# Two-sided feed-forward and delta-rule attention on one core: the order of four kinds of TensorE work in the expert tiles, and of two ScalarE steps

## The reference

```
scores = softmax(norm(x) @ gate_w)                 # 8 experts, the two best are kept
xs = scale[e, t] * norm(x)[t]                      # per expert
h  = silu(xs @ w1[e]) * (xs @ w3[e])               # 256 -> 128
out = sum over e of h @ w2[e]                      # 128 -> 256
```

## Time and profile before

| what | value |
|---|---|
| median of 3 runs | 1615.22 us (1611.40 to 1615.74) |
| span of the profiled execution, first to last instruction | 1613.1 us |
| the profiled execution's own time | not given apart from its span; the median is 2.1 us above the span |
| first mixture of experts, passes | about 146 to 263 us and 273 to 390 us |
| attention | about 390 to 1333 us |
| second mixture of experts, passes | about 1362 to 1481 us and 1490 to 1613 us |
| mean granted clock of TensorE over the span | 0.909 |

### The profile page before, as it was taken

One profiled execution on the slowest core, in us unless ns is written; L12 is line 12 of the kernel. 1 busy time (PEld: TensorE's weight loads), 2 busy tenths in 40 slices (PEclk: granted clock), 3 DMA queues, 4 the chain that ended last, 5 costly groups with the idle time before them and its releaser, 6 DMA issues. The chain is left out here.

```text
span 1613.1 us, 36942 instructions
## 1 busy us (share of the span) xinstructions
PE 1332.5 (83%) x11688; PEld 1246.2 (77%) x11688; DVE 1153.0 (71%) x3044; ACT 918.2 (57%) x1853; POOL 1004.1 (62%) x1783
## 2 busy tenths in 40 slices
PE   7673994994579999999999999999999851995996
PEld 7673994994468888888888888888888741995896
DVE  6664673673768888879889888798898534673574
ACT  2113772771356676767676767666676413772773
POOL 4762673565366676777776866867768532575366
PEclk8555997998689999999999999999999975998999
DMA  7426976772011212132222231222222245885682
GB/s 209 155 100 175 307 261 220 236 252 68 10 30 39 51 45 70 39 77 72 67 68 50 65 76 39 77 65 66 75 50 59 68 119 163 263 270 185 247 287 85
DMA packets 224026, 195.90 MB, mean 121 GB/s; under 512 B 105556, under 2 KB 186714, under 8 KB 223840
## 3 DMA queue, kind: packets, MB, share of 16 engines
q1 hardware_dynamic: 190560, 117.21, 26.4%
q0 software_dynamic: 24576, 67.94, 11.5%
q10 hardware_dynamic: 8704, 8.39, 1.8%
HBM read 103.68 MB, written 96.10 MB: 124 GB/s over the span
## 5 line engine op out<-in xcount | busy, mean ns | idle before, releaser
L1560 DVE SCALAR_TENSOR_TENSOR raw_w<-attn_raw,taps,raw_w 128x256 f32<-128x256 f32 x576 | 251.8, 496 | 43.4 <-ACT raw_w L1933 43.4
L468 PE MATMUL ffn_both<-ws,ffn_xhi 128*128 x1152 | 203.7, 289 | 0.8 <-issue 0.2
L468 PEld LDWEIGHTS ffn_both<-ws,ffn_xhi 128*128 128x128 f32 x1152 | 164.1, 192 | 3.2 <-issue 3.1
L457 PE MATMUL ffn_both<-ident,ffn_xb 128*128 128x128 f32 x576 | 82.1, 290 | 96.0 <-ACT ffn_xb L752 96.0
L2217 POOL TENSOR_TENSOR attn_inv<-attn_inv,attn_term 64x14 f32<-64x14 f32 (+6 forms) x448 | 135.5, 303 | 35.1
L2214 POOL TENSOR_TENSOR attn_term<-attn_small,attn_inv 64x14 f32<-64x14 f32 (+6 forms) x448 | 130.4, 291 | 35.1
L1201 PE MATMUL attn_fr<-attn_xhi,wqkv 128*128 128x256 f32 x768 | 149.0, 297 | 2.5 <-DVE attn_xlo L1540 1.6
L457 PEld LDWEIGHTS ffn_both<-ident,ffn_xb 128*128 128x128 f32 x576 | 70.0, 150 | 98.3 <-ACT ffn_xb L752 77.4
L1201 PEld LDWEIGHTS attn_fr<-attn_xhi,wqkv 128*128 128x128 f32 x768 | 113.4, 194 | 14.4 <-issue 10.9
L491 PE MATMUL ffn_yb<-ws,ffn_hhi 128*128 x576 | 118.6, 290 | 6.2 <-DVE ffn_hlo L667 6.2
L829 POOL DMA_INDIRECT second_rows<-ffn_more_rows,ffn_to x64 | 63.1, 986 | 85.0 <-DVE ffn_to L652 68.9
(11 more groups left out here) (319 smaller groups left out, 4139.6 us busy)
## 6 DMA issues: line engine op xcount, KB each, us to landing
ffn_more_rows<-second_rows SPq DMA_DIRECT2D x56, 259.0 KB
ffn_xb<-second_rows SPq DMA_DIRECT2D x48, 259.0 KB
raw_w<-second_rows SPq DMA_DIRECT2D x40, 259.0 KB
ffn_more_rows<-first_rows SPq DMA_DIRECT2D x64, 131.0 KB
ffn_xb<-in_L_attn_x_dram SPq DMA_DIRECT2D x8, 1024.0 KB, 5.9
attn_xin<-x_after_first ACTq DMA_DIRECT2D x32, 256.0 KB, 2.7
attn_xres<-x_after_first SPq DMA_DIRECT2D x32, 256.0 KB, 3.0
x_after_attention<-attn_xres SPq DMA_DIRECT2D x32, 256.0 KB, 2.2
```

Of the source, the lines that this page charges most:

```text
L457: last = pe.transpose(tr[:, q, j * P:(j + 1) * P], xs[:, k % 2, j, q * P:(q + 1) * P], ident[:])
L468: last = pe.matmul(hp[:, j, :], (xhi, xlo)[b][:, k % 2, q, j * P:(j + 1) * P], ws[:, bass.ds(experts[j], 1), a, q].rearrange("p o d -> p ( ...
L1560: dve.scalar_tensor_tensor(acc[:, j, r], raw[:, j, r, :, tap:tap + P], taps[:, j, r, tap:tap + 1], acc[:, j, r], ALU.mult, ALU.add)\
```

## The change

On TensorE `down(k-1)` is issued directly behind `up(k)`, and `turn_rows(k+2)` behind it, directly ahead of `turn_hidden(k)`. On ScalarE `high_hidden(k)` is issued ahead of `scaled(k+3)`. The functions themselves, the waits in them, the buffers and the other engines' orders stay as they are.

```diff
@@ -521,10 +521,10 @@   (TensorE)
                 for k in range(start, end):
                     now = table_row(k, 0, mybir.EngineType.PE, E - 1)
                     up(k, now)
+                    if k > start:
+                        down(k - 1, of)
                     if k + 2 < end:
                         turn_rows(k + 2)
-                    if k > start:
-                        down(k - 1, of)
                     turn_hidden(k)
                     of = now
                 down(end - 1, of)
@@ -795,9 +795,9 @@   (ScalarE)
                     silu(k)
                     if k + 2 < end:
                         high_part(k + 2)
+                    high_hidden(k)
                     if k + 3 < end:
                         scaled(k + 3)
-                    high_hidden(k)
                     if first_stage and 11 <= k < 16:
                         round_attention_weights(k)
```

## The result

| | kernel before | changed kernel |
|---|---|---|
| median, four runs each on one chip | 1614.42 us (1611.40 to 1615.74) | 1623.11 us (1622.25 to 1626.77) |
| ratio | | 1.0056, 95% interval 1.0037 to 1.0075 |
| profiled execution | span 1613.1 us | 1622.95 us, span 1621.2 us |
| mean granted clock of TensorE over the span | 0.909 | 0.905 |

The change costs 8.7 us by the medians and 8.1 us by the spans. That is slower by more than the 0.3% which a measurement of this kernel can tell.

What follows compares the result with a forecast made beforehand. TensorE's own work, 5.556 us a pass, was taken to bound the expert stages; 56 waits of 0.105 us make 5.9, less 0.7 of small waits 5.2, so 1615.2 + 5.2 = 1620.4 us, range 1615 to 1626.

Steps and rivals of the forecast that it cites:

- The ring: Loop down(k-1), turn_rows, high_part, low_part, low_hidden, down(k): 5.66 us against TensorE's 5.556, so 0.105 us wait ahead of down.
- The two links that no row of before showed in just this place: VectorE's low_hidden starts 0.09 us before low_part's end; hlo's end to down's first product on TensorE takes 0.20 us.
- The places: Expected signs: xlo directly behind xhi, VectorE idle ahead of xlo and not hlo, TensorE waiting about 0.1 us at down.
- One sign: TensorE idle ahead of L491 (down), about 0.1 us x 56, and a bit under 40.00 in a 40 us window.
- No overlap on VectorE: Rival: low_hidden starts only at low_part's end or 0.03 after; ring 5.75 to 5.78, 1625 to 1627 us; chance 0.12.
- The ring's own forecast: Ring of 5.62 to 5.71 us a pass, total 1618.5 to 1623, centred at 1620.4; chance 0.63.
- No new wait: Rival: hlo to down under 0.10 us, ring at or under TensorE's 5.556, time 1614.5 to 1615; chance 0.17.
- faster: Rival: TensorE saves by products directly behind products and turns behind turns; 0.08 us a pass gives 1610 us; chance 0.05.
- The clock: Rival: TensorE's clock falls with twelve turns in one block; one pass in ten costs 34 us, 1650; chance 0.03.
- How many passes: TensorE waits at downs 1 to 14 of each half: 4 x 14 x 0.105 = 5.9 us, less 0.7, 5.2.
- the slack of ScalarE's edit: Hid done at 1.63, wanted by turn_hidden at 2.39: slack 0.76 us, about 0.2 where attention weights are rounded; no cost.
- the chain of the prediction: ScalarE after the edit: xhi, hhi, four scalings ending at 6.07, silu starting at 5.97, 0.31 us into the next pass.

Runs made afterwards that it cites:

- Experiment 3: Changed kernel with low_hidden(k) ahead of goals(k+2) and low_part(k+2) on VectorE: 1765.7 us, ratio 1.0059, stalled session; repeated without stalls, 1618.44 us, ratio 1.0029.
- `pe_only`: Kernel before with TensorE's edit alone: 1772.8 us in one run, against 1753.1 of the kernel before, in a stalled session.
- Experiment 5: Changed kernel with a 128 x 256 memset added on VectorE between low_part(k+2) and low_hidden(k): 1772.3 us in one run, against 1741.3 of the kernel before, stalled session.
- `after_dve_2`: Second run of Experiment 3's kernel, in a session without stalls: 1618.44 us, ratio 1.0029 to the kernel before.
- experiment 7: Changed kernel with low_hidden ahead of low_part and the next pass's table read directly behind up(k), without stalls: 1611.03 us against 1614.01 before, ratio 0.9985.
- `act_only`: Kernel before with ScalarE's edit alone, run twice in stalled sessions (kernel before 1741 to 1753 us): 1768.4 us, ratio 1.0087, and 1764.3 us, ratio 1.0133.

## Why the prediction was right, and where it fell short

**The ring: right.** The sum was 5.66 us a pass. The trace has 5.63 and 5.67, and each link stands within 0.05 us of its term. The two links that no row of before showed in just this place came out as taken. Low_hidden started 0.07 to 0.09 us ahead of low_part's end in all 64 such pairs, and hlo to down was 0.20. The predicted loss was 5.2 us, and the ring's share is 5.3. Experiment 3 took it away by opening the ring at VectorE, and `pe_only` gave the other length, 6.99. Experiment 5 put a dose into it and moved its last links.

**The places: right.** Xlo stands directly behind xhi in time, VectorE is idle ahead of xlo (0.74 us) and not ahead of hlo, the clock is 1.00 in the windows. One sign was read wrongly beforehand. The prediction looked for idle time ahead of L491 and for TensorE a bit under 40.00 of 40. The page shows 6.2 us before and after, and two of the windows show 40.00: the trace shows the waiting first product of down as running, for 0.38 us in place of 0.28. The pitch behind it and the count of matmuls in a window show the wait.

**The rivals.** No overlap on VectorE would have made 5.75 to 5.78 us a pass; the second choices show 5.63 to 5.68 in nearly all passes. That the total comes near the first end of this rival's 1625 to 1627 us is chance: its mechanism isn't in the trace. The range of 1615 to 1626 reaches that high because of this rival. The ring's own forecast, 1618.5 to 1623, ends where the measured 1623.1 lies, so that the number came out inside the range is in part luck: 3.5 of the 8.7 us come from what wasn't in the sum. The prediction set against its sum a sentence of the Trainium skill (VectorE: DVE Perf Modes, "The DRAIN you can't avoid"), that the next VectorE operation doesn't start until the pipe is empty. The 64 early starts are for the exception that the page makes for an operation that isn't held. No new wait, and faster, fall with the 5.65. The clock didn't fall with twelve turns in a row.

**The total: short by 3.5 us** (5.2 predicted, 8.7 measured). Two steps failed. The first is "How many passes": 4 x 14 waits of 0.105 us at down, as if these were all. The chain that it counts runs through instructions on tiles. The sequencer's read of the expert's number ahead of up isn't in it, nor among the rivals. That read begins only when hid is done, and it has 0.35 us of slack; the kernel before had as little (the read below, from 213.4, ends at 213.76, and up comes at 214.45, 0.69 later, of which 0.37 are needed).

```profile
L345 PEldq TENSOR_LOAD <-tab x1: 358/358/358, 213.4 to 213.4; - x1
```

So in most passes the change didn't shorten the slack. With it more reads are long: 3 over 0.68 us before, and 10 and 12 in the two profiles of the changed kernel, 11 in that of `after_dve_2`.

The second step is the slack of ScalarE's edit: 0.76 us, and "about 0.2 us of slack stays" where the attention weights are rounded. These sizes are right for turn_hidden: hid ends 0.79 us ahead of it, and 0.13 in passes 12 and 14. But the read waits for hid too, and from hid's end to up it needs 0.06 + 0.33 + 0.37 = 0.76 us, where turn_hidden needs 0.36. For the read the slack is 0.35 to 0.4 us, and in these two passes hid comes 0.65 later, which is more than that.

That a read behind hid makes the long passes is shown: with the read a pass ahead they are gone (experiment 7 against `after_dve_2`), those with a long read and those with a late hid. Together they are 1.7 us in the stretches of the changed kernel. How the 1.7 divides is estimated above from the rows of single passes; no run separates the two. Why more reads are long is open. In the kernel before 9 of the 72 reads began while POOL was issuing a store, in the changed kernel 57, among them all ten long ones, with 11 or more of the 16 DMA engines busy. But none of the three long reads of before began in a store, 18 reads of the changed kernel took up to 0.35 us with 13 or more engines busy, and in experiment 7, with 54 reads in stores, only three are long. Traffic may be a part of the cause and isn't shown to be.

The rest, 8.1 - 7.0 = 1.1 us of the spans, lies outside the stretches. From up(16) of the second half to up(1) of the third, where the attention's code is unchanged, it took 1006.86 us before, 1008.54 after, and 1008.87, 1005.82 and 1008.20 in three other kernels. That varies by 3 us among kernels with the same code there, so this rest isn't given a cause. The last 0.6 us are between spans and medians (8.1 and 8.7).

**ScalarE's edit: its cost by itself is open.** The prediction gave it none, alone or with the other edit. Silu does stand 0.10 us later in the passes of the ring, directly behind the scalings, as the chain of the prediction has it, and that costs nothing. The rounding behind the scalings costs what the paragraph above says, and which of the two edits brings this about wasn't tried: `act_only` ran in stalled sessions alone. There it took 0.9 and 1.3% more than the kernel before, and the cause isn't known. Late rows aren't it. Nor was the kernel before run with only the early read of the table; whether its own few long passes (5.80 and 5.81 us, one in each half of first choices) and its last passes can be shortened by that edit alone is open.

## What to carry to other kernels

When work on the bounding engine is reordered, its own sum staying the same is not enough. Look for the loop that the new order closes through the other engines, and add up its links. Here it was 2% longer than the engine's work, and each pass paid the difference. Opening the loop at another engine (low_hidden ahead of low_part) gave all of it back.

A register read in an engine's queue is a link as well. Where it waits behind an instruction whose input comes late, move it a step ahead; its duration is not a constant. And slack has to be counted to every reader of a tile: here the turns had 0.4 us more than the read that stood behind the same wait.

The time from issuing a load to using its data doesn't say when the data landed. The packets do, and here they took the blame from the rows.

A busy share of 100% (40.00 us of 40 here, with 342 matmuls in place of 348) doesn't prove that an engine isn't waiting. Count its instructions in a window.

## What the runs showed of the hardware that wasn't expected

- The read of a table entry into TensorE's registers took 0.33 us at its shortest and up to 1.15 us, four numbers of one table each time. It took over 0.4 us in 9 of 72 passes before and in 35 of 72 in the changed kernel. Where up waited for it, the next product came 0.37 us behind its end.
- Going from products to turns or back cost nothing that can be read: passes with two changes of kind fewer were 5.56 us like those of before, once the ring was open.
- The same kernel took 1614 us in some sessions and 1741 to 1753 us on three other chips. In the traces from there the rows landed as soon as elsewhere (2 to 5 us from the issue), and ScalarE scaled them 12 to 30 us later in place of 2 to 12. The cause isn't known.
